# A low-pass filter kernel: the column half one step further behind the row half

## The reference

```
xs  = gelu(x @ W1.T + b1)            # 768 -> 192 channels, exact gelu
xs  = | lowpass(xs) |                # 2-D FFT over the 64x64 pixels, a centred square
                                     # of frequencies kept, inverse FFT, real part, abs
out = x + xs @ W2.T + b2             # 192 -> 768 channels
```

## Time and profile before

| | |
|---|---|
| median of 3 runs | 2421.06 us (2419.39 to 2422.68) |
| the profiled execution, whole | 2429.68 us |
| its span, first to last instruction | 2427.9 us |
| mean granted clock of PE | 0.981 |
| DVE, ACT busy | 63%, 52% |
| DMA | 710.44 MB, mean 293 GB/s |

### The profile page before, as it was taken

How to read it: one execution, slowest core, us unless ns; L and a number is a source line. 1 busy time by engine, 2 the same in 40 slices (tenths; PEclk the granted TensorE clock), 3 DMA queues, 4 the chain that set the end, 5 groups by cost and what they waited for, 6 DMA issues and landing times. The chain is left out here.

```text
span 2427.9 us, 49359 instructions
## 1 busy us (share of the span) xinstructions
PE 2326.2 (96%) x15200; PEld 2287.9 (94%) x15200; DVE 1528.7 (63%) x3101; ACT 1258.7 (52%) x3076; POOL 1477.5 (61%) x1908
## 2 busy tenths in 40 slices
PE   7899999999999999999999999999999999999977
PEld 6899998999999999999999999999999999999966
DVE  6566665666656666666665666666566666666633
ACT  4555554554545555555554555555455555555522
POOL 4666665665656666566665656666565666666522
PEclk9999999999999999999999999999999999999989
DMA  7789898888979899898888988888889898999775
GB/s 200 223 290 315 296 309 277 307 299 299 313 272 315 307 308 313 280 314 301 301 298 296 312 293 306 295 309 307 276 306 310 297 313 296 316 305 309 274 246 203
DMA packets 349045, 710.44 MB, mean 293 GB/s; under 512 B 35154, under 2 KB 233810, under 8 KB 348756
## 3 DMA queue, kind: packets, MB, share of 16 engines
q1 hardware_dynamic: 348756, 707.06, 85.5%
HBM read 455.26 MB, written 251.66 MB: 291 GB/s over the span
## 5 line engine op out<-in xcount | busy, mean ns | idle before, releaser
L550 DVE TENSOR_TENSOR xc<-ps,xc 128x384 f32<-128x384 f32 x1024 | 571.4, 558 | 673.2 <-PE ps L374 658.5
L589 POOL TENSOR_TENSOR hid_lo<-hid,hid_hi 128x384 fp32r<-128x384 f32 x256 | 258.7, 1011 | 526.3 <-issue 300.0
L411 ACT ACTIVATE xt_hi<-ps 128x384 fp32r<-128x384 f32 x512 | 247.5, 483 | 555.1 <-PE ps L298 555.0
L320 PE MATMUL ps<-w1v,vt_hi 128*128 128x384 f32 x1536 | 492.9, 371 | 17.0 <-POOL vt_lo L604 10.2
L320 PE MATMUL ps<-w1e,xt_hi 128*128 128x384 f32 x1536 | 499.0, 374 | 0.1
L604 POOL TENSOR_TENSOR vt_lo<-vt,vt_hi 128x768 fp32r<-128x768 f32 x256 | 470.8, 1839 | 18.5 <-ACT vt_hi L416 18.5
L436 ACT ACTIVATE oa_hi<-y 128x256 fp32r<-128x256 f32 x256 | 107.1, 418 | 569.8 <-issue 510.5
L321 PE MATMUL ps<-w1v,vt_lo 128*128 128x192 f32 x1536 | 387.9, 253 | 0.0
L321 PE MATMUL ps<-w1e,xt_lo 128*128 128x192 f32 x1536 | 387.5, 252 | 0.0
L366 PE MATMUL ps<-w2a_hi,oa_hi 128*128 128x384 f32 x1024 | 380.9, 372 | 0.7 <-DVE xc L550 0.7
L512 DVE TENSOR_TENSOR xt_lo<-ps,xt_hi 128x384 fp32r<-128x384 f32 x512 | 275.6, 538 | 134.0 <-ACT xt_hi L411 134.0
(11 more groups left out here) (60 smaller groups left out, 4255.9 us busy)
## 6 DMA issues: line engine op xcount, KB each, us to landing
xc<-x_dram SPq DMA_DIRECT2D x256, 768.0 KB, 7.2
out_dram<-xc SPq DMA_DIRECT2D x256, 768.0 KB, 5.5
xv<-x_dram SPq DMA_DIRECT2D x1024, 96.0 KB, 2.6
xe<-x_dram SPq DMA_DIRECT2D x256, 384.0 KB, 4.3
filtered_rows<-filt SPq DMA_DIRECT2D x256, 192.0 KB, 3.7
cols<-filtered_rows SPq DMA_DIRECT2D x128, 384.0 KB, 7.8
xc<-w1t_dram SPq DMA_DIRECT2D x4, 144.0 KB, 3.9
xc<-w1t_dram SPq DMA_DIRECT2D x1, 576.0 KB, 7.3
```

The lines of the kernel that those rows point to most:

```text
L320: nc.tensor.matmul(ps_h[t][:, 0:2 * D], hi, w1s[:, k, :], start=k == 0, stop=False)
L550: nc.vector.tensor_tensor(x_half, ps_o[u % 2][:, 0:HALF], x_half, ALU.add).then_inc(s_add, 1)
L589: nc.gpsimd.tensor_tensor(hid_lo[:, q % 2, :, :], hid[:, q % 2, :, :], hid_hi[:, q % 2, :, :].bitcast(F32), ALU.subtract).then_inc(s_hlo, 1)
```

## The change

`FILTER_H` goes from 18 to 19, and with it `OUT` to 20 and `STORE` to 21. The first chunk of an image is still read in step 17 (`READ_COLS` stays 17 while `FILTER_H` moves), but after the row write of that step, behind `all_rows_written`, both now last in SP's step. The other chunks are read in the steps they were read in before, which is now three steps ahead of their use and not two. The corner sums and their copy stay in step 17 (`CORNER`), where now the last pair of the previous image is still to come: so the table is held twice, by the parity of the image, the sums wait for one pair less, and the height filter's last pair waits for the copy. SP's steps are all written out in line.

```diff
-FILTER_H = PAIRS + 2
+FILTER_H = PAIRS + 3
 OUT = FILTER_H + 1
 STORE = OUT + 1
-READ_COLS = FILTER_H - 1
+READ_COLS = FILTER_H - 2
+CORNER = PAIRS + 1
...
-        corner = sb("corner", [P, 3, 8])
+        corner = sb("corner", [P, 2, 3, 8])
...
-                    if (at := stage(i, s, READ_COLS)) and at[1] == 0:
-                        all_rows_written(at[0])
                     if at := stage(i, s, OUT - XC_LEAD):
                         load_xc(*at)
-                    if (at := stage(i, s, READ_COLS)) and (at[1] == 0 or at[1] % 2 == 1 and at[1] < PAIRS - 1):
+                    if (at := stage(i, s, READ_COLS)) and at[1] % 2 == 1 and at[1] < PAIRS - 1:
                         read_cols(at[0], (at[1] + 1) // 2)
                     if at := stage(i, s, LATE):
                         write_rows(*at)
-
-            turns(sp, turn)
+                    if (at := stage(i, s, READ_COLS)) and at[1] == 0:
+                        all_rows_written(at[0])
+                        read_cols(at[0], 0)
+
+            turns_in_line(turn)
...
             def corner_sums(m):
                 pe.wait_ge(s_acc, PAIRS * (m + 1))
                 until(pe, s_corner, 1, m, 0)
-                until(pe, s_y, PAIRS, m, 0)
+
+                until(pe, s_y, PAIRS, m, -1)
...
                 if r == 0:
                     until(pe, s_corner, 1, m, 1)
+                if r == PAIRS - 1 and m + 1 < IMAGES:
+
+                    pe.wait_ge(s_corner, m + 2)
...
-                        if j == 2 and (at := stage(i, s, FILTER_H - 1)) and at[1] == 0:
+                        if j == 2 and (at := stage(i, s, CORNER)) and at[1] == 0:
                             corner_sums(at[0])
...
             def corner_copy(m):
                 until(dve, s_cmm, 1, m, 1)
-                until(dve, s_y, PAIRS, m, 0)
-                nc.vector.tensor_copy(corner[:].rearrange("p g n -> p (g n)"), ps_corner[:]).then_inc(s_corner, 1)
+                until(dve, s_y, PAIRS, m, -PAIRS)
+                nc.vector.tensor_copy(corner[:, m % 2].rearrange("p g n -> p (g n)"), ps_corner[:]).then_inc(s_corner, 1)
...
-                    if (at := stage(i, s, READ_COLS)) and at[1] % 2 == 0:
+                    if (at := stage(i, s, FILTER_H - 1)) and at[1] % 2 == 0:
                         pack_cols_b(at[0], at[1] // 2)
```

More of the change, by code:

```diff
@@ L176, in next_pair @@
             return m + 1, 0
[L178 to L185, removed]
         def turns_in_line(turn):
@@ L538, in y_pair @@
                     until(dve, s_corner, 1, m, 1)
-                table = corner[:].rearrange("p g (a n) -> p g a n", a=1).to_broadcast([P, 3, 16, 8])
+                table = corner[:, m % 2].rearrange("p g (a n) -> p g a n", a=1).to_broadcast([P, 3, 16, 8])
                 nc.vector.tensor_tensor(y[:, r % 2, :, :].rearrange("p g (a n) -> p g a n", n=8),
```

## The result

| | before | after |
|---|---|---|
| median, runs side by side | 2421.87 us | 2352.54 us |
| lowest to highest | 2419.39 to 2422.75 | 2352.11 to 2355.42 |
| ratio, 95% interval | | 0.9718 [0.9701, 0.9735] |
| span of the profiled execution | 2427.9 us | 2350.3 us |
| mean granted clock of PE | 0.981 | 0.994 |

The change saves 69 us, or 2.8%. The forecast was 2367 us, the range 2354 to 2388. The direction and the mechanism at the boundary were right; the gain was put 14 us too small and the median lies just under the range.

What follows compares the result with a forecast made beforehand. PE bounds the kernel step by step, losing time at image boundaries to late column reads and slow clock. -57.7 - 8.8 (one full step less) + 1.1 + 8.0 = -57.4 us gives 2372.3 profiled; median forecast 2367 us, range 2354 to 2388.

Steps and rivals of the forecast that it cites:

- Boundary loss: At 14 boundaries between images, PE's 75.5 us loss falls to 17.8 us (1.27 each): 57.7 us go.
- It lands 7.8 us later: First column read, issued behind step 17's row write, lands 7.8 us later, 10.6 at worst; in time for the pack.
- first rival, late reads: First chunk lands late at most boundaries, idling PE 1 to 1.5 us each: +20 us, 2387 us; chance 0.12.
- SP in line: I count 0, with at most 1 us a boundary: Writing SP's steps in line gains 0, at most 1 us a boundary either way; SP waits 3.5 us a step for ACT.
- the 0.61 of the earlier trace: DMA share just before a boundary, read as queues that had run empty by themselves with PE full.
- the DMA rival: Without pauses, DMA cannot hold the 312 GB/s wanted and every step grows: at 297 GB/s, 2471 us; chance 0.03.
- The second corner table ... cost nothing: Second corner table, waits for one pair less and the last pair's new wait add 0 us.
- Tail: From the last image's first pair, four intervals totalling 30.5 us replace 22.5 us: +8.0 us; the last 15 intervals stay.
- the lower bound of +3: Low bound of the tail's term, if a step behind no slow clock is shorter; the upper bound was +10.
- the 3.01 us waits: PE's idle time before even pairs in the tail: POOL's late pack, not a late column read, so it stays.
- Head: One more row-only step of some 5.2 us at the start puts the second height filter at 129.1, not 128.03: +1.1 us.
- The 8.6 us between profile and median: Profiled execution's excess over the median run; a little over half was taken to go, within 2363.7 to 2372.3 us.

Runs made afterwards that it cites:

- unshifted: The changed kernel with its second corner table declared behind all other tiles, so y to ob1 lie as in the kernel before: 2363.71 us, step 8.826 us.
- cover taken: The changed kernel with all column reads one step later, the extra lag kept: 2399.14 us, ratio 0.9899.
- experiment 6: The changed kernel with POOL's pack ahead of the low parts: 2332.23 us; then also two running corner sums: 2321.99; then also other tile places: 2314.64.
- read_last_18: The kernel before (lag 18) with SP in line and the first chunk's read last in SP's step: 2392.75 us, ratio 0.9868.

## Why the prediction was wrong

On the two profiled executions the forecast was -57.4 us and the measured -77.6, 20.2 us more: 9.3 from the length of a step, 5.0 from the tail, 3.8 from the head, 2.1 from the boundaries. On the medians it was 14.5 us more, as the forecast had put 5.3 us of the first profile's excess on waits that go. The step that failed first is the term of the second corner table, which the prediction put at nothing: without its 9.3 us the time lies in the forecast's range, as unshifted shows with 2363.71 us.

- **Boundary loss: right.** Forecast 57.7 us, measured 59.8. What stays is 1.12 a boundary and not 1.27. That isn't the place of the tiles, as unshifted, with the old place, keeps 1.12 too; where the 0.15 sat was not traced. The size came out right with an incomplete reason, which is luck in part: the prediction had no cause for the late reads, and SP in line alone would have ended nearly all of these waits as well (next but one).
- **"It lands 7.8 us later": mis-sized.** It is 3.8 to 5.1 us for the reads of the changed kernel's profile that follow a quiet SP (3.7 to 6.0 in its second profile). The median of all reads was taken for one in an unusual place of the queue. It cost nothing here, as it only made the slack larger, but it is why "cover taken" was put 80 us too high. What the Trainium skill says on load, in "DMA: Bandwidth & Descriptors", section "Latency and other measured facts", fits in direction: the median read rose from 7.8 to 8.2 us as the mean rate rose from 293 to 302 GB/s. That the latency of HBM did it no run here shows. The first rival, late reads, did not occur: no wait of PE for `cols`.
- **"SP in line: I count 0, with at most 1 us a boundary": the step that failed as a reason.** The argument was SP's mean slack of 3.5 us a step, "so its instruction stream isn't on the path in either form". The loop's cost sits in one step of 16, as a gap of 3 to 5 us, and in the one step where SP's timing matters. Alone it is worth 46 us (2425.53 to 2379.76). It doesn't show in the error of the sum, since the lag's cover removes the same waits: beside the lag it is 1.4 us (2355.02 to 2353.67). So the 0 was right as a term and wrong as an account of the kernel before. Two rows of the kernel before spoke against it. SP's sequencer waited 35.8 us for the row writes at the ends of the images (2.9 with SP in line alone):

```profile
SPq L238 <- DMA filtered_rows<-filt: 35.8, 15, 3.4
```

And the 0.61 of the earlier trace rows, which the prediction read as DMA queues that had run empty by themselves, is the gap: SP issues nothing from 384.45 to 388.48. Of the same window, before the gap and in it (the columns of the earlier trace rows):

```profile
380.00:384.44 4.44, 4.44 (x32) 4.41 (x31) 3.07 (x8) 2.83 (x8) 3.76 (x5) 1.00 0.95 365
384.44:388.48 4.04, 4.04 (x29) 4.01 (x29) 2.75 (x5) 2.05 (x4) 1.95 (x5) 1.00 0.36 133
```

The forecast's argument against the DMA rival fell with that; that the rival did not occur, the 311 GB/s after show.

- **"The second corner table ... cost nothing": the largest term of the miss.** It moved the tiles behind it and made a full step 0.04 us shorter, 9.3 us in all, where the prediction had said that steps bound by PE can hardly differ. No row of the kernel before could have shown it. As an unknown it belonged in the range: the placements tried here span 18 us.
- **Tail: +8.0 forecast, +3.0 measured.** The four intervals are 7.0, 7.4, 5.4 and 7.8 us, 27.6 in place of 30.5, all at granted clock 1.00; I took 5.9 and 8.6 from rows at clocks of 0.71 and 0.96, and named the lower bound of +3 without using it. The last 15 and the end took 2.1 us less than before. Between the second profiles of both kernels the tail's term is +4.6. That the 3.01 us waits are POOL's order and stay was right, and experiment 6 shows it.
- **Head: +1.1 forecast, -2.7 measured.** Start-up differs by as much from one execution to the next: the second height filter stands at 128.03 and 126.26 in two profiles of the kernel before, at 125.37 and 128.41 in two of the changed one.
- **The 8.6 us between profile and median.** I put half of them on waits that go. Another profile of the kernel before has a span of 2421.9 us with nearly the same boundary losses (74.5 us by the same count); it differs by 1.8 us in the head and 3.3 in the tail. So the excess was that execution's own, in parts that stay, and the sum made on the median, 2363.7, would have been 3 us nearer.

## What to carry to other kernels

A mean slack says nothing on a cost that comes once an iteration: look at the step in which a loop branches back, and at what is due in that step. Before buying cover with another stage of lag, ask what makes the transfer late, and where periodic work falls by parity. And give some of the range to any edit that changes a tile's size: here placement alone spans 0.8% of the time.

## What the runs showed of the hardware

- SP stood still 2.9 to 5.5 us at each of 48 back edges in four profiles of a long hardware loop, against 0.24 us at the same place in other steps. An 8 KB instruction packet started 1.78 to 1.95 us before the end of each of these gaps.
- A 384 KB read landed in 3.6 to 5.2 us where SP had issued only a row write in the 6 us before it (28 boundaries of cover_taken and read_last_18), and in 7.0 to 9.3 us right behind a step's loads (14 of SP in line alone). The 192 KB write ahead of it landed in 2.0 to 3.5 us in line and in 5.7 to 8.6 us behind loads that a back edge had delayed.
- The same instructions on PE ran at 8.757 to 8.834 us a step, at granted clock 1.00, by where tiles of a few KB lay in SBUF.
